# A chip kernel's gathers in two bursts: seven groups, a pause, and then gathers and scatters in turn

## The chip, the cores and the metric

The kernel runs on one core of a Trainium2 chip. The metric is the device time of one execution, in microseconds (us). The engines are PE (matrix products and transposes), ACT, DVE (elementwise work), POOL (here above all the indirect DMAs, each of which POOL issues itself) and SP, whose queue issues the plain DMAs.

## What is computed

`x` has 8192 rows of 256 numbers. The whole is a feed-forward layer with its own attention and a mixture of experts, then a causal self-attention, then the same feed-forward layer again:

```python
x = x + 0.5 * _L0_ffn_ref(_layernorm(x), ...)     # first ffn
x = x + _L0_attn_ref(_layernorm(x), ...)
x = x + 0.5 * _L0_ffn_ref(_layernorm(x), ...)     # second ffn
```

Inside the feed-forward layer, after its attention (`y1`), each row goes to one of 8 experts:

```python
idx = argmax(softmax(y1 @ wg)); loc = position of the row within its expert; keep = loc < cap
h = disp @ w1 + b1;  y = h @ w2 + b2              # per expert, no nonlinearity between
out = where(keep, gate * y[slot], 0)
y2 = layernorm(y1 + out) * ln2_g + ln2_b
```

With nothing nonlinear between `w1` and `w2`, an expert is one 256 x 256 matrix, the product W1W2, and one bias row.

## The kernel before, in words

`ffn` is called twice, with `turn` 0 and 1; the change touches the call with `turn` 0. Each call has three stages.

First `ffn_attention` runs over 16 groups (NG) of 512 rows and stores, for each row, the rows `y1` and `x + ln2_b` side by side in the DRAM scratch `rows`. Then comes the routing: DVE works out each row's slot, and PE turns that into the inverse permutation `inv` (a chain that ends with `s_inv`). In the first call alone, the eight experts' products are formed here too, and go on after the routing is done. Per expert e: PE transposes w1 (`turn_w1`, L1235), ACT copies it out of PSUM (`turned`, L1116), PE multiplies with w2 (`product`, L1246, 32 matmul records), ACT stores the product (`w12_out`, L1121), DVE sums the bias (`bias_product`, L1436 and L1439), PE spreads that sum over the partitions (`bias_sum`, L1277) and DVE adds it (`bias_out`, L1427). `s_w12ps` counts PE's products and `s_acc` DVE's bias sums.

The third stage is the tail, 16 groups of 4 x 128 rows sorted by expert. `gather(n)` issues four indirect DMAs from POOL (L1083) that bring rows of `rows` into `xs[:, n]`; ACT copies them (`place`), PE transposes and multiplies with W1W2 (`products`, L1318), DVE adds and takes the row statistics (`sums`, L1454 to L1473), ACT normalises (L1165), and DVE scales with `ln2_g` and adds (`scale`, L1486 and L1489), which counts up `s_fin`. POOL then scatters the group with four indirect DMAs (L1101) to the place of each row in the output. The stage that follows starts when the last scatter has landed.

The order on each engine is that in which the code is written. On POOL all sixteen gathers stand ahead of all scatters. The buffer `xs` is shared: while the products are formed, the parts 10 and 11 of it hold w1 and the parts 12 to 15 hold w2. Therefore gathers 10 and 11 wait for transposes of w1 (`s_etps`), and gathers 12 to 15 for product and bias sum number n - 7. Each gather from the third on also waits until the one two before it has landed (`got`).

Of the kernel before, what the change touches and what calls it, by code (L numbers as in the profile page):

```python
# [32 lines left out]
NE = 8  # L33
# [898 lines left out]
def ffn(core, name, x, rows, d, w12d, b12d, out, turn, tables):  # L932
# [4 lines left out]
    FB = FF // P  # L937
    CT = TILES // NG * 2
    MINE = (3, 7)
    with Phase(core, name) as ph:  # L940
        logits = ph.sb("logits", [P, TILES, NE])

# [127 lines left out]
        @block.gpsimd  # L1070
        def _(pool):
            nc.gpsimd.iota(ei[:, :], pattern=[[1, NE]], base=0, channel_multiplier=0).then_inc(s_iota, 1)
            nc.gpsimd.iota(ib[:, :], pattern=[[1, P]], base=0, channel_multiplier=0).then_inc(s_ib, 1)
            nc.gpsimd.iota(ni[:, :], pattern=[[1, TILES]], base=0, channel_multiplier=TILES).then_inc(s_ni, 1)
            nc.gpsimd.memset(zero[:, :], 0.0).then_inc(s_zero, 1)
            attend_gpsimd(pool)

            def gather(n):
                if n >= 2:
                    got(pool, n - 2, n % 2)  # L1080
                for t in range(GT):
                    i = n * GT + t
                    pool.indirect_dma_start(xs[:, n, t, :], None, rows,  # L1083
                                            bass.IndirectOffsetOnAxis(ap=inv[:, i:i + 1], axis=0)
                                            ).then_inc(s_got[n % 2], 16)

            for u in range(2):
                stored(pool, u)
            pool.wait_ge(s_inv, 1)
            for n in range(NG):  # L1090
                if turn == 0 and n in (10, 11):
                    pool.wait_ge(s_etps, 4 * (n - 3))
                if turn == 0 and n >= 12:
                    pool.wait_ge(s_w12ps, n - 7)
                    pool.wait_ge(s_acc, n - 7)
                gather(n)
            for n in range(NG):
                pool.wait_ge(s_fin, n + 1)
                for t in range(GT):
                    i = n * GT + t  # L1100
                    pool.indirect_dma_start(out, bass.IndirectOffsetOnAxis(ap=inv[:, i:i + 1], axis=0),  # L1101
                                            xs[:, n, t, 0:C], None).then_inc(s_sent, 16)
            pool.wait_ge(s_sent, sent0 + 16 * TILES)

        @block.scalar
# [1364 lines left out]
```

## Time and profile before

| | us |
|---|---|
| median of 3 runs | 2764.93 |
| lowest and highest | 2763.07 and 2767.3 |
| the profiled execution's own time | 2759.59 |
| its span (first to last instruction) | 2757.9 |
| PE busy in the span | 2334.6 |
| DVE busy | 2151.4 |
| ACT busy | 1657.1 |
| POOL busy | 838.6 |

The first call's routing, products and tail lie between about 488 and 756 us of the span, the second call's tail between 2546 us and the end. A timeline row of the profile gives the start, the length, the engine, the line, the operation and, in brackets, how long the engine was idle before it and what ended that idle time. "issue" there is idle time for which the profile shows nothing that was waited for, and "remote" is a release that it cannot put to an engine of this core.

### The profile page before, as it was taken

The numbers are of one execution on the slowest core, as the hardware profiler recorded it, in microseconds if no ns is written. First come the engines' busy times: TensorE is split into PE (matmuls) and PEld (weight loads), VectorE is DVE, ScalarE is ACT, GpSimd is POOL, SyncE is SP. The second block draws the span as 40 slices with busy tenths as digits, with TensorE's granted clock in tenths as the row PEclk, the third lists the DMA queues.
The fourth block names the chain that finished last, engine by engine and source line by source line (L and its number), as shares of the span: only waits on it lengthen the run. The fifth ranks groups of instructions, "written<-read, shape, count | busy, mean of one in ns | idle before, by whom it ended". The sixth has DMA issues, their size and how long they took to land. (4 is left out here: it accounts for less than half of the span.)

```text
span 2757.9 us, 45893 instructions
## 1 busy us (share of the span) xinstructions
PE 2334.6 (85%) x15352; PEld 1387.7 (50%) x15352; DVE 2151.4 (78%) x5653; ACT 1657.1 (60%) x3995; POOL 838.6 (30%) x853
## 2 busy tenths in 40 slices
PE   5999998877479969999999999999879999994264
PEld 3666665755345524444444444444656666663243
DVE  5888887827778869889889898888458888887077
ACT  3454544416534429999999999999415445452154
POOL 2353433264734430000000000000123343431746
PEclk8999999878889969999999999999989999997677
DMA  4132214283235565445455455452441121211722
GB/s 122 52 97 77 70 47 145 102 271 115 84 126 172 168 126 103 94 102 108 95 106 106 94 105 104 96 107 60 130 153 54 47 69 47 69 47 52 210 73 77
DMA packets 244683, 281.54 MB, mean 102 GB/s; under 512 B 41808, under 2 KB 212880, under 8 KB 243808
## 3 DMA queue, kind: packets, MB, share of 16 engines
q1 hardware_dynamic: 217712, 218.02, 31.1%
q0 software_dynamic: 16384, 50.35, 5.7%
q10 hardware_dynamic: 10352, 10.23, 1.3%
q8 instruction: 123, 2.02, 0.3%
q14 instruction: 112, 0.92, 0.1%
HBM read 190.63 MB, written 94.16 MB: 103 GB/s over the span
## 5 line engine op out<-in xcount | busy, mean ns | idle before, releaser
L2202 DVE CUSTOM_DVE_ANT_0 banks<-banks,attn_bias 128x128 f32<-128x128 f32 (+7 forms) x1024 | 759.7, 778 | 108.1 <-PE banks L1909 82.8
L2115 ACT ACTIVATE attn_probT<-banks 128x512 f32<-128x512 f32 x1152 | 622.5, 621 | 61.2 <-PE banks L1926 50.9
L1909 PE MATMUL banks<-attn_kst,attn_qst 96*128 96x512 bf16 (+3 forms) x1536 | 421.4, 336 | 22.3 <-DMA attn_qst<-qparts 12.3
L1926 PE MATMUL banks<-attn_qst,attn_kst 99*128 99x256 bf16 (+3 forms) x2176 | 410.9, 281 | 15.3 <-ACT attn_probT L2115 7.1
L1948 PE MATMUL banks<-attn_probT,attn_vb 128*32 128x256 f32 (+3 forms) x4352 | 315.6, 400 | 7.9 <-ACT attn_probT L2115 7.3
L1926 PEld LDWEIGHTS banks<-attn_qst,attn_kst 99*128 99x128 bf16 x2176 | 187.3, 97 | 169.3 <-ACT attn_probT L2115 54.9
L2260 POOL CAST attn_lowp<-attn_lowT 128x32 bf16<-128x32 f32 x64 | 13.4, 209 | 850.3 <-DVE attn_lowT L2210 850.3
L410 PE MATMUL banks<-ffn_xT,winT 128*128 128x512 f32 x512 | 250.7, 612 | 6.5 <-ACT ffn_w L610 2.9
L1909 PEld LDWEIGHTS banks<-attn_kst,attn_qst 96*128 96x128 bf16 x1536 | 117.4, 97 | 255.6 <-DVE attn_low L2202 158.1
L2103 ACT COPY banks<-attn_biasT 128x512 f32<-128x512 f32 x384 | 227.8, 628 | 27.9 <-DMA attn_biasT<-neardT 21.2
L870 POOL TENSOR_TENSOR ffn_xs<-ffn_xs,row_ffn_out 128x1024 f32<-128x1024 f32 x32 | 75.4, 2356 | 412.3 <-DVE ffn_xs L752 386.5
L580 ACT ACTIVATE ffn_xs<-banks,ffn_xs 128x128 f32<-128x128 f32 x512 | 182.5, 379 | 12.9 <-DVE ffn_xs L717 11.4
L1948 PEld LDWEIGHTS banks<-attn_probT,attn_vb 128*32 128x32 f32 x4352 | 106.2, 109 | 132.8 <-ACT attn_probT L2115 70.1
L619 ACT COPY ffn_xs<-banks 128x256 f32<-128x256 f32 x128 | 48.2, 377 | 205.3 <-PE banks L459 202.8
L1318 PE MATMUL banks<-ffn_w,ffn_xT 128*128 128x256 f32 x512 | 130.3, 408 | 43.0 <-issue 30.7
L1083 POOL DMA_INDIRECT ffn_xs<-rows,ffn_inv x128 | 122.7, 958 | 141.5 <-DVE ffn_inv L1423 90.5
L610 ACT ACTIVATE ffn_w<-banks,ffn_qk_b 64x512 f32<-64x512 f32 x128 | 87.3, 682 | 125.7 <-PE banks L410 124.9
L717 DVE TENSOR_REDUCE ffn_xs<-banks 128x4 f32<-128x512 f32 x128 | 88.4, 691 | 86.8 <-PE banks L439 86.5
L2202 DVE DVE_READ_ACCUMULATOR2_ANT attn_low<- 128x1 f32 x1024 | 143.8, 140 | 0.1
L725 DVE TENSOR_SCALAR ffn_xs<-ffn_xs 128x128 f32<-128x128 f32 x512 | 138.4, 332 | 4.5
L439 PE MATMUL banks<-ffn_w,ffn_xs 128*128 128x256 f32 x512 | 141.1, 400 | 0.8 <-DVE ffn_xs L739 0.8
L410 PEld LDWEIGHTS banks<-ffn_xT,winT 128*128 128x128 f32 x512 | 90.3, 192 | 93.3 <-issue 73.8
(254 smaller groups left out, 4507.9 us busy)
## 6 DMA issues: line engine op xcount, KB each, us to landing
rows<-ffn_xs SPq DMA_DIRECT2D x64, 512.0 KB, 3.1
attn_qst<-qparts SPq DMA_DIRECT2D x384, 64.0 KB, 2.8
attn_kst<-kparts SPq DMA_DIRECT2D x186, 128.0 KB, 5.0
ffn_xs<-in_L_ffn_w_dram SPq DMA_DIRECT2D x16, 1024.0 KB
attn_biasT<-neardT SPq DMA_DIRECT2D x128, 128.0 KB, 5.0
attn_bias<-neard SPq DMA_DIRECT2D x128, 128.0 KB, 2.2
qparts<-qkv_part SPq DMA_DIRECT2D x32, 384.0 KB, 2.8
kparts<-qkv_part SPq DMA_DIRECT2D x32, 384.0 KB, 2.8
```

What stands on the lines that cost most here:

```text
L410: mm = nc.tensor.matmul(bank[QK], core.winT[:, k, j * P:(j + 1) * P], xT[:, u, k, :], start=(k == 0), stop=(k == KB - 1))
L439: mm = nc.tensor.matmul(bank[SC[t % 2]][:, 2 * j * P:(2 * j + 2) * P].rearrange("p (h c) -> p h c", h=2), qT[:, u, j, t * P:(t + 1) * P], ...
L580: ins = nc.scalar.activation(prob[:, t % 2, h, :], bank[SC[t % 2]][:, h * P:(h + 1) * P], ACT.Exp, bias=negm[:, t % 2, h:h + 1], scale=1.0 ...
L725: ins = nc.vector.tensor_scalar(prob[:, t % 2, h, :], prob[:, t % 2, h, :], rinv[:, t % 2, h:h + 1], None, ALU.mult)
L1083: pool.indirect_dma_start(xs[:, n, t, :], None, rows, bass.IndirectOffsetOnAxis(ap=inv[:, i:i + 1], axis=0)).then_inc(s_got[n % 2], 16)
L1318: mm = nc.tensor.matmul(part, xT[:, u, k, t * P:(t + 1) * P], w12[:, k, expert(n, u)], start=False, stop=(k == KB - 1), skip_group_check=True)
L1909: mm = nc.tensor.matmul(score[k % 2][:, a:e], qst[0:K6, u, half, hh, ii * P:(ii + 1) * P], kst[0:K6, u, hh, a:e], start=True, stop=True)
L1926: mm = nc.tensor.matmul(tbank[t % 3][:, at:at + nb * P], kst[:, u, hh, j * P:(j + 1) * P], qst[:, u, half, hh, x:x + nb * P], start=(k == ...
L1948: mm = nc.tensor.matmul(obank[32 * hh:32 * hh + 32, x:x + nb * P], vb[:, u, j, hh, :], probT[:, g % 2, i, at:at + nb * P], start=hh not in ...
L2103: nc.scalar.copy(tbank[t % 3].rearrange("p (a c) -> p a c", a=2), over(near[:, 0:2 * P], 2, 1)).then_inc(s_seed, 1)
L2115: nc.scalar.activation(probT[:, g % 2, i, 0:w], tbank[t % 3][:, 0:w], ACT.Exp, scale=-1.0).then_inc(s_exp, 1)
L2202: nc.vector.tensor_tensor_reduce(out=part, in0=part, in1=bias[:, hh, T - w:T], scale=1.0, scalar=BIG, op0=ALU.add, op1=ALU.min, accum_out= ...
```

## The change

In the first call the gathers of groups 0 to 6 are issued as before. Then POOL waits for the eighth product and the eighth bias sum. After that it issues the gathers of groups 7 to 12, scatter 0, gather 13, scatter 1, gather 14, scatter 2, gather 15, scatter 3, and then scatters 4 to 15. The waits of gathers 10 to 15 on single transposes and products go away, since the one wait covers them. In the second call `AHEAD` is 16, and its order is as before.

```diff
     CT = TILES // NG * 2
     MINE = (3, 7)
+    AHEAD = (12, NG)[turn]
...
-            for u in range(2):
-                stored(pool, u)
-            pool.wait_ge(s_inv, 1)
-            for n in range(NG):
-                if turn == 0 and n in (10, 11):
-                    pool.wait_ge(s_etps, 4 * (n - 3))
-                if turn == 0 and n >= 12:
-                    pool.wait_ge(s_w12ps, n - 7)
-                    pool.wait_ge(s_acc, n - 7)
-                gather(n)
-            for n in range(NG):
+            def scatter(n):
                 pool.wait_ge(s_fin, n + 1)
                 for t in range(GT):
                     i = n * GT + t
                     pool.indirect_dma_start(out, bass.IndirectOffsetOnAxis(ap=inv[:, i:i + 1], axis=0),
                                             xs[:, n, t, 0:C], None).then_inc(s_sent, 16)
+
+            for u in range(2):
+                stored(pool, u)
+            pool.wait_ge(s_inv, 1)
+            for n in range(NG):
+                if turn == 0 and n == 7:
+                    pool.wait_ge(s_w12ps, NE)
+                    pool.wait_ge(s_acc, NE)
+                gather(n)
+                if n >= AHEAD:
+                    scatter(n - AHEAD)
+            for n in range(NG - AHEAD, NG):
+                scatter(n)
             pool.wait_ge(s_sent, sent0 + 16 * TILES)
```

On POOL, before the change, these rows are gathers 9 to 12 of the first call; each group is one row with its waits (`indirect0` and `indirect1` are the landings of earlier gathers) and one row for its other three DMAs.

```order
L1083 DMA ffn_xs<-rows,ffn_inv 128x512 [waits indirect1]
L1083 DMA ffn_xs<-rows,ffn_inv 128x512 x3
L1083 DMA ffn_xs<-rows,ffn_inv 128x512 [waits indirect0,ffn1_etps]
L1083 DMA ffn_xs<-rows,ffn_inv 128x512 x3
L1083 DMA ffn_xs<-rows,ffn_inv 128x512 [waits indirect1,ffn1_etps]
L1083 DMA ffn_xs<-rows,ffn_inv 128x512 x3
L1083 DMA ffn_xs<-rows,ffn_inv 128x512 [waits indirect0,ffn1_acc,ffn1_w12ps]
L1083 DMA ffn_xs<-rows,ffn_inv 128x512 x3
```

On POOL after the change, gathers 6 to 8 of the first call:

```order
L1084 DMA ffn_xs<-rows,ffn_inv 128x512 [waits indirect0]
L1084 DMA ffn_xs<-rows,ffn_inv 128x512 x3
L1084 DMA ffn_xs<-rows,ffn_inv 128x512 [waits indirect1,ffn1_acc,ffn1_w12ps]
L1084 DMA ffn_xs<-rows,ffn_inv 128x512 x3
L1084 DMA ffn_xs<-rows,ffn_inv 128x512 [waits indirect0]
L1084 DMA ffn_xs<-rows,ffn_inv 128x512 x3
```

The wait on the product and the bias sum has moved from gather 12 to gather 7, and it is now for number 8, where gather 12 waited for number 5; no gather behind it has such a wait.

The second place is the end of the gathers on POOL. Before, it is gather 15 and then scatters 0 and 1:

```order
L1083 DMA ffn_xs<-rows,ffn_inv 128x512 [waits indirect1,ffn1_acc,ffn1_w12ps]
L1083 DMA ffn_xs<-rows,ffn_inv 128x512 x3
L1101 DMA x<-ffn_xs,ffn_inv 8192x256 [waits ffn1_fin]
L1101 DMA x<-ffn_xs,ffn_inv 8192x256 x3
L1101 DMA x<-ffn_xs,ffn_inv 8192x256 [waits ffn1_fin]
L1101 DMA x<-ffn_xs,ffn_inv 8192x256 x3
```

After the change, on POOL, it is gather 12, scatter 0, gather 13, scatter 1 and gather 14:

```order
L1084 DMA ffn_xs<-rows,ffn_inv 128x512 [waits indirect0]
L1084 DMA ffn_xs<-rows,ffn_inv 128x512 x3
L1092 DMA x<-ffn_xs,ffn_inv 8192x256 [waits ffn1_fin]
L1092 DMA x<-ffn_xs,ffn_inv 8192x256 x3
L1084 DMA ffn_xs<-rows,ffn_inv 128x512 [waits indirect1]
L1084 DMA ffn_xs<-rows,ffn_inv 128x512 x3
L1092 DMA x<-ffn_xs,ffn_inv 8192x256 [waits ffn1_fin]
L1092 DMA x<-ffn_xs,ffn_inv 8192x256 x3
L1084 DMA ffn_xs<-rows,ffn_inv 128x512 [waits indirect0]
L1084 DMA ffn_xs<-rows,ffn_inv 128x512 x3
```

Scatter 0 has moved ahead of gathers 13 to 15, which thereby stand behind its wait on `s_fin`. The rows of the other engines stand in the same order before and after.

## Rows read from the trace of the kernel before

**Rows 1.** Busy time by stretch: engines, granted PE clock, DMA share, GB/s.

```profile
core 0: us, PE busy (x) PEld busy (x) DVE busy (x) ACT busy (x) POOL busy (x), PEclk, DMA share, GB/s
580.00:590.00 10.00, 6.20 (x13) 3.10 (x13) 0.00 (x0) 0.00 (x0) 7.56 (x9) 0.50 0.76 242
590.00:600.00 10.00, 3.99 (x7) 2.06 (x7) 0.00 (x0) 0.58 (x1) 7.01 (x8) 0.50 0.72 210
```

**Rows 2.** Timeline of PE during the products of the first call.

```profile
546.96 7.07 PE L1246 MATMUL banks<-ffn_xs,ffn_xT 128*128 128x256 f32 x32
...
584.77 1.98 PE L1246 MATMUL banks<-ffn_xs,ffn_y 128*128 128x256 f32 x3
...
601.59 6.74 PE L1246 MATMUL banks<-ffn_xs,ffn_y 128*128 128x256 f32 x18 [0.81 <-issue]
...
608.60 7.07 PE L1246 MATMUL banks<-ffn_xs,ffn_xT 128*128 128x256 f32 x32
```

**Rows 3.** Timeline of POOL: gathers of the first call.

```profile
539.34 1.44 POOL L1083 DMA_INDIRECT ffn_xs<-rows,ffn_inv  x1 [46.62 <-DVE ffn_inv L1423]
...
578.20 0.95 POOL L1083 DMA_INDIRECT ffn_xs<-rows,ffn_inv  x1 [0.30 <-issue]
...
598.19 0.94 POOL L1083 DMA_INDIRECT ffn_xs<-rows,ffn_inv  x1 [0.30 <-issue]
603.42 0.94 POOL L1083 DMA_INDIRECT ffn_xs<-rows,ffn_inv  x1 [4.29 <-remote]
...
622.68 0.95 POOL L1083 DMA_INDIRECT ffn_xs<-rows,ffn_inv  x1 [0.30 <-issue]
628.45 0.94 POOL L1083 DMA_INDIRECT ffn_xs<-rows,ffn_inv  x1 [4.82 <-issue]
```

**Rows 4.** Timeline of ACT: copies of products out of PSUM.

```profile
598.10 0.58 ACT L1121 COPY ffn_w<-banks 128x512 f32<-128x512 f32 x1 [23.41 <-remote]
...
620.56 0.59 ACT L1121 COPY ffn_w<-banks 128x512 f32<-128x512 f32 x1 [9.72 <-remote]
```

**Rows 5.** Timeline of DVE: bias sums of the products.

```profile
603.23 0.43 DVE L1427 TENSOR_TENSOR ffn_b<-banks,ffn_b 128x256 f32<-128x256 f32 x1 [24.06 <-remote]
...
623.38 0.42 DVE L1427 TENSOR_TENSOR ffn_b<-banks,ffn_b 128x256 f32<-128x256 f32 x1 [10.24 <-remote]
...
624.10 3.61 DVE L1439 SCALAR_TENSOR_TENSOR ffn_acc<-ffn_xs,b1T,ffn_acc 128x256 f32<-128x256 f32 x7
```

**Rows 6.** Timeline of DVE in the first tail.

```profile
653.81 1.23 DVE L1489 TENSOR_TENSOR ffn_xs<-ffn_xs 128x1024 f32<-128x1024 f32 x1
...
659.07 1.22 DVE L1486 TENSOR_TENSOR ffn_xs<-ffn_xs,row_ln_g 128x1024 f32<-128x1024 f32 x1
660.32 1.22 DVE L1489 TENSOR_TENSOR ffn_xs<-ffn_xs 128x1024 f32<-128x1024 f32 x1
...
743.78 1.24 DVE L1489 TENSOR_TENSOR ffn_xs<-ffn_xs 128x1024 f32<-128x1024 f32 x1
```

**Rows 7.** Timeline of POOL: scatters of the first tail.

```profile
655.32 1.01 POOL L1101 DMA_INDIRECT x<-ffn_xs,ffn_inv  x1 [22.17 <-DVE ffn_xs L1489]
...
659.19 1.94 POOL L1101 DMA_INDIRECT x<-ffn_xs,ffn_inv  x1 [0.30 <-issue]
...
742.49 0.97 POOL L1101 DMA_INDIRECT x<-ffn_xs,ffn_inv  x1 [0.30 <-issue]
...
755.23 0.97 POOL L1101 DMA_INDIRECT x<-ffn_xs,ffn_inv  x1 [0.30 <-issue]
```

**Rows 8.** Timeline of POOL, second tail: first and last of 64 gathers.

```profile
2547.20 1.09 POOL L1083 DMA_INDIRECT ffn_xs<-rows,ffn_inv  x1 [43.92 <-DVE ffn_inv L1423]
...
2626.12 0.94 POOL L1083 DMA_INDIRECT ffn_xs<-rows,ffn_inv  x1 [0.30 <-issue]
```

**Rows 9.** Timeline of DVE in the second tail.

```profile
2571.35 0.87 DVE L1460 SCALAR_TENSOR_TENSOR ffn_xs<-banks,ffn_gnow,ffn_xs 128x256 f32<-128x256 f32 x2
2592.01 0.88 DVE L1460 SCALAR_TENSOR_TENSOR ffn_xs<-banks,ffn_gnow,ffn_xs 128x256 f32<-128x256 f32 x2 [19.79 <-remote]
...
2634.77 0.17 DVE L1454 COPY ffn_gnow<-ffn_gates 128x4 f32<-128x4 f32 x1 [39.83 <-remote]
```

## The prediction, made before the changed kernel had run

> **What bounds the kernel now.** I read the shares by stretch first, because the change touches one engine's order in one stage, and what matters is what each engine does between the end of the routing (538 us) and the end of the first tail (756 us). From 580 to 600 us [rows 1] POOL issues gathers at full pace, while DVE has no instruction and ACT one. PE runs 20 matmuls in these 20 us, at the 1.2 GHz level of its clock (0.50), and the DMA engines are not full (0.72 to 0.76). So neither a busy engine nor bandwidth holds these 20 us.
>
> The timelines of the engines say what it is. A product of 32 matmuls takes 7.07 us at 547 and at 608 us; the one begun at 584.77 ends only at 608 us [rows 2], over 23 us. ACT's store of a product comes at 598.10 after 23.41 us idle [rows 4]; DVE's next bias add comes at 603.23 after 24.06 us idle [rows 5]. "Issue" and "remote" mean that no engine's work was late. What does fit is the gather stream: POOL issues the 44 gathers of groups 0 to 10 from 539.34 and ends the last at 599.13, waits 4.29 us itself, and goes on at 603.42 [rows 3]. DVE and PE are back to full pace within the same four microseconds. It recurs: the 16 gathers of groups 11 to 14 run from 603.42 to 623.63, ACT's last store waits from the product's end (608.60 + 7.07 = 615.67) to 620.56, and DVE's bias add until 623.38 [rows 2 to 5]. The second tail shows it at its largest: 64 gathers in a row from 2547.20 to 2627.06 [rows 8], and DVE stands 19.79 and 39.83 us in them, until 2634.77 [rows 9]. I read this as: a long unbroken stream of gathers stops the other engines' instructions after a while, and they come back about 4 us (7.7 after the long stream) after it ends.
>
> The tail itself is bound by DVE: group 0 is finished at 655.04, group 1 at 661.54, so 6.5 us a group, and group 15 at 745.02 [rows 6]. POOL's last scatter ends at 756.20 [rows 7], and the next stage waits for it.
>
> **The change, step by step** (in the profiled execution's own time).
>
> *The pause.* Gather 27, the last of group 6, ends at 578.20 + 0.95 = 579.15 [rows 3]. Ending there takes 16 gathers out of the stream, 1.25 us apart (578.20 to 598.19 is 16 of them). If the engines recover 4 us later, as at 603, they are back at 583.2. The bounds are 579 (at once) and 586.9 (7.7 us). From there PE does the end of the bias sum (0.7), the product (7.07), a bias sum (0.4), the last product (7.07) and a bias sum (0.6): 599.0. DVE follows with one bias add (0.4) and the last bias product, which before began 0.34 us after 623.38 and ended at 624.10 + 3.61 = 627.71 [rows 5], 4.33 us in all: 603.3. So the eighth bias sum moves from 627.7 to 603.3, 24.4 us earlier (20.7 to 28.5). ACT's copies (0.6 each) and SP's two stores of the products to DRAM lie beside this; the stores then flow while POOL is silent or in its first gathers.
>
> *What is behind the new wait.* Gathers 7 to 15 and with them every scatter. POOL starts 0.74 us after the bias sum, as it did at 628.45: 604.0. Six groups are 24 gathers x 1.25 = 30 us, to 634.0. Before, only gather 15 was still to be issued at this point. This is the price of the pause: 32 more gathers, 40 us of POOL's time, lie behind that point.
>
> *The tail's start.* DVE finished group 0 at 655.04, 27.3 us after the last bias sum; unhindered that is 630.6. Scatter 0 could then go at 634. But from 604 to 634 POOL streams gathers without a break. In the second tail, which also began after a rest, DVE stopped at 2572.2, 25 us after the first gather [rows 8, 9]. The same here is 629, just short of group 0's end. POOL then stands at scatter 0's wait from 634 on, the stream is broken, 4 us later (638) the engines are back, and group 0's last steps take 2 to 3 us. I take scatter 0 at 641; the ends are 635 (no stop, and DVE in POOL's way once) and 655 (rival C).
>
> *From scatter 0 to the end.* POOL now has 16 scatter groups and 3 gather groups, one after another: 16 x 5.10 (the ten steps from 742.49 to 755.23 are 1.274 each [rows 7], so 5.10 a group) + 3 x 5.0 = 96.6 us. The scatter at 659.19, which started 0.12 us into DVE's two-input multiply, took 1.94 us instead of 0.97; that at 742.49, started just before one, took 0.97 [rows 6, 7]. So each of some 14 groups that DVE still finishes may cost POOL nothing to 1.0 us; I take 12 us in all, with 0 and 14 as the ends. That is 108.6 us from scatter 0 to the last scatter's end, where before it was 756.20 - 655.32 = 100.9. DVE, at 6.5 us a group, needs only 90 us from group 0 to group 15, so POOL is the bound, and a stop of DVE by up to 15 us in the middle would be hidden.
>
> The Trainium skill, page "SBUF — State Buffer", section "Who interferes with whom", says that a DVE instruction with two SBUF inputs contends only with a GpSimd instruction that reads SBUF, and supposes that writing descriptors needs the other interface. By that the twelve microseconds would be 0 and the end that much earlier. The scatter at 659.19 doubled, and our gathers and scatters read their indices from SBUF, so the trace decides for the cost.
>
> *Sum.* 641 + 108.6 = 749.6 against 756.2: 6.6 us less. The stages behind only move. From the profiled execution's 2759.6 this gives 2753.0; the median of the runs is 2764.9, 5.3 above it, and I carry the difference over: **2758.3 us**.
>
> **The rivals.**
>
> *A, no second stop.* Scatter 0 goes at 635, and the end is 635 + 108.6 = 743.6, 12.6 us less: 2752.3. For it: group 0 needs only until 630.6, and DVE in the second tail still worked 25 us after the first gather. Against it: that same 25 us.
>
> *C, the second burst stops the tail for long.* In the first call the second stream made ACT late after 12.3 us (603.42 to 615.67), though after a rest of only 4 us. If DVE stops 12.3 us into the new burst, at 616.3, then 14.3 us of work remain before group 0 is done (630.6); the engines return at 638 to 641.7, so scatter 0 goes at 652.3 to 656: the end is 761 to 765, that is 5 to 8 us slower, around 2771.5. A further stop under the alternating stream, beyond the 15 us of cover, would come on top. It decides from the point where scatter 0 comes later than 756.2 - 108.6 = 647.6; the burst itself is over at 634.
>
> *D, the gathers are not what stops the engines.* Then the last bias sum stays at 627.7, gather 7 starts at 628.4, scatter 0 at 628.4 + 30 + 1 = 659.5, and the end is 768, 12 us slower: 2776.8. For it: at 547 a product takes its 7.07 us beside gathers. Against it: three stops, each ending within 8 us of a stream's end. The Trainium skill, page "SBUF — State Buffer", section "SBUF: two separate sides", says that a DMA cannot be slowed by a compute instruction nor the reverse; by that rule this rival would hold and its 12 us with it. The trace disagrees as far as a product of 23 us beside gathers, against 7.07, can show it.
>
> *E, gain and price cancel for another reason*, such as scatters that land late: 2764.9.
>
> **How the numbers follow.** A change of 0.2% is 5.5 us, about what a measurement of this kernel can tell from none. The forecast (a short second stop, 1 to 10 us gained) has 0.42, its own range 2755 to 2764; 0.25 of it is faster and 0.17 the same. A has 0.21, faster. C has 0.23: 0.07 the same, 0.16 slower. D has 0.12, slower, and E 0.02. Together 0.46 faster, 0.26 the same, 0.28 slower. Leaving out D with the far end of C (0.14) and A's far end, where the recovery is instant and DVE costs POOL nothing (0.05), the range is 2749 to 2773.
>
> **What would show it.** Right: PE runs both last products at 7.07 us from about 583; the eighth bias sum ends near 603; POOL idles about 24 us after gather 6 and is then never idle over 2 us from scatter 0 on; DVE's group 15 is done some 20 us before POOL's last scatter. The second stop shows as "remote" on DVE or ACT between 622 and 640 and as POOL's wait ahead of scatter 0. Wrong if PE still has its gaps from 583 to 601 with POOL silent (D), if DVE stands over 12 us in the burst (C), or if scatter 0 goes at 635 (A). Most exposed is the length of the second stop: each microsecond of it beyond 634 is one of the sum.

## The result, and the profile after

| us | before | changed |
|---|---|---|
| median of 6 runs each, on one chip | 2766.11 | 2773.59 |
| lowest and highest | 2758.11 and 2768.0 | 2772.57 and 2778.2 |
| the profiled execution's own time | 2759.59 | 2773.26 |
| its span | 2757.9 | 2771.5 |
| PE / DVE / ACT / POOL busy | 2334.6 / 2151.4 / 1657.1 / 838.6 | 2338.3 / 2153.6 / 1657.3 / 836.2 |
| last scatter of the first tail ends | 756.20 | 767.92 |

The changed kernel is slower: the ratio is 1.0032, with the 95% interval 1.0022 to 1.0041. The busy times are the same within 4 us, so no work was added. Of the 13.6 us by which the span is longer, 11.7 are there when the first tail ends. The second call's code is unchanged, and its tail is nearly so: 202.6 us for 203.2, with stops of DVE of 19.66 and 36.82 us for 19.79 and 39.83 [rows 9].

These are rows of POOL's timeline in the changed kernel: the gathers (L1084) and scatters (L1092) of the first call at which something begins or ends.

```profile
577.58 0.94 POOL L1084 DMA_INDIRECT ffn_xs<-rows,ffn_inv  x1 [0.30 <-issue]
601.53 0.95 POOL L1084 DMA_INDIRECT ffn_xs<-rows,ffn_inv  x1 [23.01 <-DVE ffn_acc L1443]
...
630.26 0.95 POOL L1084 DMA_INDIRECT ffn_xs<-rows,ffn_inv  x1 [0.30 <-issue]
645.91 1.01 POOL L1092 DMA_INDIRECT x<-ffn_xs,ffn_inv  x1 [14.71 <-DVE ffn_xs L1493]
...
652.36 1.88 POOL L1084 DMA_INDIRECT ffn_xs<-rows,ffn_inv  x1 [0.30 <-issue]
...
681.86 0.97 POOL L1092 DMA_INDIRECT x<-ffn_xs,ffn_inv  x1 [0.31 <-issue]
692.87 0.97 POOL L1092 DMA_INDIRECT x<-ffn_xs,ffn_inv  x1 [10.04 <-DVE ffn_xs L1493]
...
766.95 0.97 POOL L1092 DMA_INDIRECT x<-ffn_xs,ffn_inv  x1 [0.30 <-issue]
```

They answer to [rows 3] and [rows 7]. POOL is silent for 23.01 us, as the new wait asks, issues the 24 gathers of groups 7 to 12 from 601.53 to 631.21, and then waits 14.71 us for DVE's group 0. From 645.91 to 682.83 it issues 28 DMAs of both kinds without a gap. Then it waits once more, 10.04 us, for DVE's group 4.

This is PE's timeline during the pause (L1250 is the product, L1281 the bias sum), and one row of the second burst and three from the end of the mixed stream of gathers and scatters.

```profile
581.58 7.07 PE L1250 MATMUL banks<-ffn_xs,ffn_y 128*128 128x256 f32 x32
...
588.92 7.07 PE L1250 MATMUL banks<-ffn_xs,ffn_xT 128*128 128x256 f32 x32
...
625.57 4.18 PE L1322 MATMUL banks<-ffn_w,ffn_xT 128*128 128x256 f32 x9 [6.52 <-issue]
...
681.69 0.38 PE L1322 MATMUL banks<-ffn_w,ffn_xT 128*128 128x256 f32 x1 [0.88 <-issue]
683.09 0.38 PE L1322 MATMUL banks<-ffn_w,ffn_xT 128*128 128x256 f32 x1 [1.03 <-issue]
684.49 0.59 PE L1322 MATMUL banks<-ffn_w,ffn_xT 128*128 128x256 f32 x1 [1.02 <-issue]
```

With POOL silent both last products take 7.07 us each, where one begun at 584.77 took over 23 us before [rows 2]. In the burst PE stands again for 6.52 us and gets through 9 matmuls in 4.18 us. The last three rows show that a "stop" is not always a standstill: PE runs single matmuls, 1.40 us apart, though nothing that the profile shows holds it.

DVE's timeline shows the rest: the last bias product, the row behind which the second stop begins, that stop's end, the last operation of group 0, and the same pair for a third stop with the end of group 4 behind it.

```profile
597.18 3.61 DVE L1443 SCALAR_TENSOR_TENSOR ffn_acc<-ffn_xs,b1T,ffn_acc 128x256 f32<-128x256 f32 x7
...
616.51 0.22 DVE L1477 TENSOR_SCALAR ffn_ve<-ffn_mv 128x4 f32<-128x4 f32 x1
634.93 0.17 DVE L1458 COPY ffn_gnow<-ffn_gates 128x4 f32<-128x4 f32 x1 [18.20 <-remote]
...
644.41 1.22 DVE L1493 TENSOR_TENSOR ffn_xs<-ffn_xs 128x1024 f32<-128x1024 f32 x1
...
652.18 1.22 DVE L1490 TENSOR_TENSOR ffn_xs<-ffn_xs,row_ln_g 128x1024 f32<-128x1024 f32 x1
...
670.54 1.23 DVE L1493 TENSOR_TENSOR ffn_xs<-ffn_xs 128x1024 f32<-128x1024 f32 x1
685.99 0.17 DVE L1458 COPY ffn_gnow<-ffn_gates 128x4 f32<-128x4 f32 x1 [14.22 <-remote]
...
691.37 1.23 DVE L1493 TENSOR_TENSOR ffn_xs<-ffn_xs 128x1024 f32<-128x1024 f32 x1
```

The eighth bias product ends at 600.79 (627.71 before). From 616.73 DVE stands 18.20 us, until 3.7 us after the burst's last gather has ended, and group 0 is done at 645.63. It stands again 14.22 us, until 3.2 us after the mixed stream's last DMA has ended at 682.83, so that group 4 is done at 692.60, 20.8 us after group 3. Not all of this is DVE's own: by the program the row at L1458 waits for PE's products of the next group, and in the third stop PE took from 676.63 to 687.76 for 16 matmuls that took 3.69 us at 663.46. Before the change DVE did stand by itself: PE's bias sum was done at 584.65, and the add that waited for it came at 603.23 [rows 5].

The busy time by stretch in the changed kernel (columns as in [rows 1]) puts the pause beside the two later stops.

```profile
580.00:601.00 21.00, 17.72 (x90) 15.47 (x90) 12.57 (x29) 6.68 (x11) 0.00 (x0) 1.00 0.23 94
616.00:635.00 19.00, 7.94 (x26) 5.10 (x25) 0.73 (x7) 3.22 (x6) 11.56 (x13) 0.77 0.66 191
662.00:683.00 21.00, 11.37 (x44) 8.71 (x43) 5.67 (x16) 7.12 (x14) 15.96 (x17) 0.76 0.49 151
```

In the pause PE runs 90 matmuls with its clock granted at the 2.4 GHz level (1.00), in place of the 20 at 0.50 before. In the second stretch the pattern of [rows 1] is back: POOL busy, all the others mostly standing. In the third it is weaker: PE is still busy 11.37 of the 21 us, DVE 5.67. The DMA engines are at 0.66 and 0.49 of their time, further from full than before. What the pause took out of the middle of the routing came back twice in the tail.

### The profile page after: what moved, and what is told of

The parts are those of the page before. It is cut to its first block and busy times, and to the rows that moved or that the text cites. A ratio compares the mean times of both kernels' runs of the same rounds, so it can differ in the third digit from the quotient of the medians.

```text
span 2771.5 us, 45886 instructions
## 1 busy us (share of the span) xinstructions
PE 2338.3 (84%) x15350; PEld 1392.6 (50%) x15352; DVE 2153.6 (78%) x5653; ACT 1657.3 (60%) x3995; POOL 836.2 (30%) x853
## 5 line engine op out<-in xcount | busy, mean ns | idle before, releaser
L2264 POOL CAST attn_lowp<-attn_lowT 128x32 bf16<-128x32 f32 x64 | 13.4, 209 | 851.0 <-DVE attn_lowT L2214 851.0
L1322 PE MATMUL banks<-ffn_w,ffn_xT 128*128 128x256 f32 x512 | 141.0, 429 | 57.4 <-issue 47.0
L1084 POOL DMA_INDIRECT ffn_xs<-rows,ffn_inv x128 | 123.2, 963 | 155.8 <-DVE ffn_inv L1427 90.7
L1322 PEld LDWEIGHTS banks<-ffn_w,ffn_xT 128*128 128x128 f32 x512 | 108.1, 217 | 82.6 <-issue 53.4
```

The lines of the kernel that those rows point to most:

```text
L1084: pool.indirect_dma_start(xs[:, n, t, :], None, rows, bass.IndirectOffsetOnAxis(ap=inv[:, i:i + 1], axis=0)).then_inc(s_got[n % 2], 16)
L1322: mm = nc.tensor.matmul(part, xT[:, u, k, t * P:(t + 1) * P], w12[:, k, expert(n, u)], start=False, stop=(k == KB - 1), skip_group_check=True)
```

## The experiments

Two theories stood first. **S**: an unbroken stream of POOL's indirect DMAs stops PE, ACT and DVE after some time, wherever in the program it runs, and they return when it ends. **P**: the stops belong to places of the program and have a length of their own. Later **W** was added: the pause is POOL time thrown away, which costs even where nothing is stopped. "Order" is the sequence of gathers and scatters on POOL. Each ratio is to the kernel before on the same chip, and where one edit is given as "the change's lines", the diff of the change stands there unaltered but for what is shown. A trace is of one execution, and executions of one kernel differ: those of e1 by 11.5 us. The traced executions of e1, e2 and e4 are slow ones (2773.15, 2777.96 and 2777.22 us, 4 to 6 above the medians), so their places in a trace are compared with the changed kernel's (2773.26) only roughly. From the first gather to the end of the last scatter the first tail takes 216.9 us before, 229.2 with the change, 230.5 in e1, 233.6 in e2, 232.8 in e3, 234.4 in e4 and 215.6 in e8.

**e1: the pause alone.** The waits of the change, and all gathers ahead of all scatters.

```diff
+    AHEAD = NG
```

> The pause alone: the wait ahead of gather 7 stays, all sixteen gathers stand ahead of the scatters again. Theory S (an unbroken gather stream stops the other engines until about 4 us after it ends): the second stream is now 36 gathers, 601.5 to 646.5 us; DVE stands from about 617 to 650, group 0 is done near 661, the tail is bound by DVE behind that, and the last scatter ends near 762 (767.9 in the changed kernel, 756.2 before): a time of about 2772. Theory P (the engines run out of instructions at fixed places of the program and the length of the stop is that of a fetch, whatever POOL does): DVE stands 18 us at the same instruction as in the changed kernel, group 0 is done near 646, last scatter near 747: a time of about 2757.

Measured: 2767.56, ratio 1.0023 [1.0011, 1.0035]. The last 36 gathers run from 602.10 to 646.9, and the last scatter ends at 767.5. These rows of e1's DVE timeline are its stops in them. (An idle time of 12.03 us that ended at 615.52 is mostly the ordinary wait for group 0's products; it is 8.51 us in e9, where nothing stops.)

```profile
625.28 0.88 DVE L1464 SCALAR_TENSOR_TENSOR ffn_xs<-banks,ffn_gnow,ffn_xs 128x256 f32<-128x256 f32 x2 [8.68 <-issue]
...
652.70 0.17 DVE L1458 COPY ffn_gnow<-ffn_gates 128x4 f32<-128x4 f32 x1 [24.49 <-remote]
```

The same work on DVE, the row at L1458, is let go at 634.93 with 24 gathers and at 652.70 with 36: the end of the stop moves with the end of the stream (+3.7 and +5.8 us). That speaks against P. The end, expected 6 us before the changed kernel's, came as late as that in this trace (767.5 and 767.9): scatter 0 goes only at 663.69, where 645.91 is the changed kernel's, and from it to the end it is 103.8 us, near the 100.9 of before. The trace is the slowest of e1's ten executions; by the medians the pause alone costs 6 us.

**e2: the turns alone.** `AHEAD` and `scatter` of the change, but the old waits of gathers 10 to 15.

```diff
             for n in range(NG):
                 if turn == 0 and n in (10, 11):
                     pool.wait_ge(s_etps, 4 * (n - 3))
...
                 gather(n)
+                if n >= AHEAD:
+                    scatter(n - AHEAD)
```

> The alternation alone: gathers 7 to 15 have their old waits, and scatters 0 to 3 stand between gathers 12 to 15. Theory S: the stop from 580 to 603 us comes back, but the stream behind 603 is only 8 gathers long, so the one of 616 to 623 falls away; the eighth bias sum comes near 620, group 0 near 648, and then the mixed stream of 16 scatters and 12 gathers stops the engines once more for about 13 us: last scatter near 769, a time of about 2779. Rival (the mixed stream stops them only because the burst came just before): no stop there, last scatter near 757, a time of about 2767.

Measured: 2774.02, ratio 1.0041 [1.0026, 1.0055], the last scatter ends at 774.4. Rows of e2's DVE and then POOL timelines:

```profile
699.23 0.17 DVE L1460 COPY ffn_gnow<-ffn_gates 128x4 f32<-128x4 f32 x1 [10.01 <-remote]
...
706.10 0.97 POOL L1092 DMA_INDIRECT x<-ffn_xs,ffn_inv  x1 [9.65 <-DVE ffn_xs L1495]
```

Without any pause, and with scatter 0 at 653.46, near the 655.32 of before, gathers and scatters in turn (653.5 to 696.5) stop DVE, and POOL then waits 9.65 us for it. This is the changed kernel's third stop without the burst ahead of it, so the rival falls, and it is the step that the prediction had taken as harmless. The turns alone cost about 11 us (0.0041 of 2762), the pause alone 6 and both together 9. The stop is not all of the 11: from scatter 0 to the end e2 takes 121.0 us for 100.9, and the twelve gathers that now stand behind scatter 0 are 15 of POOL's time by themselves.

**e3: half the bytes.** The change's lines, and the gathers of groups 7 to 15 fetch rows of 1 KB, half their size. It leaves out the second half of those rows (ln2's shift and the residual); the computation behind goes on with zeros or old numbers there.

```diff
+                half = turn == 0 and n >= 7
...
-                    pool.indirect_dma_start(xs[:, n, t, :], None, rows,
+                    pool.indirect_dma_start(xs[:, n, t, 0:C] if half else xs[:, n, t, :], None, x if half else rows,
```

> The changed kernel, with gathers 7 to 15 of the first call fetching 1 KB a row (from x) in place of 2 KB (from rows), so that the second half of those groups is not loaded; the number of DMAs, of rows and of descriptors is the same. If bytes moved make the stop, none or a much shorter one comes in the second burst (24 gathers) and in the mixed stream: scatter 0 near 632, last scatter near 741, a time of about 2746. If the number of gathers or rows makes it, DVE stands about 18 and 14 us as in the changed kernel and the time stays near 2773.

Measured (one run): 2777.69, the last scatter ends at 773.0. Rows of e3's DVE timeline:

```profile
626.38 0.88 DVE L1469 SCALAR_TENSOR_TENSOR ffn_xs<-banks,ffn_gnow,ffn_xs 128x256 f32<-128x256 f32 x2 [7.97 <-remote]
...
639.16 0.17 DVE L1463 COPY ffn_gnow<-ffn_gates 128x4 f32<-128x4 f32 x1 [9.85 <-remote]
...
697.57 0.17 DVE L1463 COPY ffn_gnow<-ffn_gates 128x4 f32<-128x4 f32 x1 [11.37 <-remote]
```

The busy time of a stretch of e3's burst, and of one of e7, where the gathers are spaced and nothing stops (columns as in [rows 1]):

```profile
618.00:632.00 14.00, 4.48 (x22) 3.77 (x21) 3.24 (x13) 1.14 (x2) 10.65 (x12) 0.71 0.37 104
...
600.00:620.00 20.00, 18.98 (x79) 13.44 (x79) 8.53 (x31) 8.85 (x16) 15.04 (x27) 0.87 0.85 292
```

The stops sum to 17.8 us in the burst, as long as the changed kernel's 18.20, at 104 GB/s and a DMA share of 0.37; in e7 PE is busy 18.98 of 20 us beside 292 GB/s and a share of 0.85. So it is not the bytes and not how full the DMA engines are. What is left is the number of DMAs, or of the rows in them, which e3 leaves as it was: these two were not told apart. Scatters, which carry 1 KB a row too, fit that.

**e4: the last three gather groups spread out.** The waits of the change, and gathers 13, 14 and 15 behind scatters 3, 6 and 9.

```diff
+                for n in range(NG):
+                    scatter(n)
+                    if n in (3, 6, 9):
+                        gather(12 + n // 3)
```

> The changed kernel with gathers 13, 14 and 15 moved behind scatters 3, 6 and 9 in place of 0, 1 and 2. POOL has the same work from scatter 0 on, but one gather group for three or four scatter groups. Theory S with a share (scatters count little): the burst's stop stays (scatter 0 near 646), the second stop goes, POOL works through in 108.6 us, last scatter near 754.5: a time of about 2760. Rival (any unbroken work of POOL stops the engines, scatters as much as gathers): a stop of some 14 us stays, somewhere in 662 to 700, last scatter at 760 to 768, a time of 2766 to 2773.

Measured: 2772.7, ratio 1.0032 [1.0018, 1.0046], the last scatter ends at 774.7. A miss: I had expected it to be as fast as before, and the rival came true. A row of e4's DVE timeline, and two of its POOL timeline:

```profile
709.90 0.17 DVE L1464 COPY ffn_gnow<-ffn_gates 128x4 f32<-128x4 f32 x1 [8.57 <-remote]
...
716.77 0.97 POOL L1092 DMA_INDIRECT x<-ffn_xs,ffn_inv  x1 [9.49 <-DVE ffn_xs L1499]
...
752.17 0.96 POOL L1092 DMA_INDIRECT x<-ffn_xs,ffn_inv  x1 [7.55 <-DVE ffn_xs L1499]
```

The stops came later and in smaller pieces, and POOL waited 9.49 and 7.55 us all the same. Scatters without a gap count as well; which of the two kinds is issued makes no difference that these runs show.

**e5, e6: two rests behind each gather DMA.** The order of before; behind each indirect DMA of a gather, POOL writes two tiles of 128 x 128 and waits for each, so that the DMAs are mostly 1.70 us apart in place of 1.25 (1.84 and 1.86 on average, since DVE and landings hold some up): in the first call (e5), in both (e6).

```diff
+            def rest(times):
+                for _ in range(times):
+                    nc.gpsimd.memset(filler[:, :], 0.0).then_inc(s_filled, 1)
+                    filled[0] += 1
+                    pool.wait_ge(s_filled, filled[0])
...
+                    if turn == 0:
+                        rest(2)
```

> The kernel before with its old order, and after each gather DMA of the first call two small POOL memsets with a wait on each, so that the gathers come some 1.7 us apart in place of 1.25. Theory B (the engines stop when POOL's DMAs have run at full pace for some 15 to 25 us; a rest of 4 to 8 us, or a share of POOL's issuing under about three quarters, keeps them free): no stop of over 5 us between 560 and 650; the eighth bias sum at about 600, gathers until about 650, scatters until about 742, a time 14 us below before. Rival N (the stops follow the number of gathers issued, not their pace): the stops stay, the gathers end 25 to 30 us later, and the time is 15 to 25 us above before.

> The same pace in both calls. Theory B: in the second tail, too, DVE no longer stands 20 and 40 us; it works at 6.5 us a group behind gathers that end about 112 us after their start (2659 on the old scale), the scatters end near 2750 in place of 2758: a time about 7 us below that of the first call's pace alone, and 20 below before. Rival N: the second tail grows by the 30 us of added POOL time.

Measured: e5 2762.97, ratio 0.9984 [0.9975, 0.9994]; e6 2763.21, ratio 0.9986 [0.9976, 0.9995]. The gather stops went as expected, the times did not: 4 us below before in both, for 14 and 20. In e5 DVE has no idle time over 6 us that ends in "remote" or "issue" while gathers are issued (539 to 656), and group 0 is done at 622.8, where it was 655.04. Only POOL is late now: the gathers end at 656, and the scatters follow without a gap. Rows of e5's DVE and then POOL timelines:

```profile
714.39 0.17 DVE L1465 COPY ffn_gnow<-ffn_gates 128x4 f32<-128x4 f32 x1 [16.95 <-remote]
...
721.45 0.97 POOL L1112 DMA_INDIRECT x<-ffn_xs,ffn_inv  x1 [11.67 <-DVE ffn_xs L1500]
```

The scatters from 657.5 to 709.8 stop DVE for 16.95 us: scatters alone do it. The stops are cured in the gathers at a price of at least 0.45 us for each of 64 DMAs, 29 us, which eats most of the gain.

**e7: one rest behind each gather DMA, both calls.** As e6 with `rest(1)`, mostly a DMA every 1.45 us (1.54 and 1.56 on average).

> Both calls, with one memset after each gather DMA: some 1.5 us apart, a share of about 0.83. Theory B: stops come later and are shorter than before but not gone; a time between before and the slower pace, 5 to 15 us below before. Rival N: 10 to 15 us above before in each call.

Measured: 2739.47, ratio 0.9893 [0.9875, 0.9911]. The first tail's gathers begin at 542.04, and the last scatter ends at 744.1: 202.1 us, where before it is 216.9 [rows 3, 7]. The second goes from 2535.7 to 2731.0, 195.3 us for 203.2. The time is 28 us below before, more than the 5 to 15 expected, and apart from the ordinary wait for group 0 DVE has no idle time of over 6.1 us left under the gathers; the stops that are left, up to 16.78 us, fall under the scatters, which have no rests. That a slower POOL makes the kernel 1% faster is the strongest sign for S.

**e8: a shorter pause.** The change's order; gather 7 waits for the seventh product only, and 12 to 15 have their old waits.

```diff
+                if turn == 0 and n == 7:
+                    pool.wait_ge(s_w12ps, NE - 1)
```

> The changed kernel, with gather 7 waiting for the seventh product (about 589) in place of the eighth and its bias sum (601), and the old waits back on gathers 12 to 15: a rest of 11 us in place of 23. Theory B (rest beyond some 8 us buys nothing): the eighth bias sum stays near 601, the second stream runs from 589 to 619 and stops DVE until about 623, group 0 is done near 641 in place of 645.6, the last scatter near 763 in place of 767.9: a time about 5 us below the changed kernel. Rival (the whole rest is needed, and each microsecond less costs one more of stop): the bias sum comes late by 5 to 10 us and the time is that of the changed kernel or above.

Measured: 2763.75, ratio 0.9991 [0.9982, 1.0001]. POOL's timeline in e8, gather 7, scatter 0, scatter 4 and the last scatter:

```profile
592.17 0.94 POOL L1084 DMA_INDIRECT ffn_xs<-rows,ffn_inv  x1 [10.60 <-PE banks L1252]
...
635.15 1.01 POOL L1092 DMA_INDIRECT x<-ffn_xs,ffn_inv  x1 [9.56 <-DVE ffn_xs L1495]
...
682.14 0.97 POOL L1092 DMA_INDIRECT x<-ffn_xs,ffn_inv  x1 [9.72 <-DVE ffn_xs L1495]
...
756.34 0.97 POOL L1092 DMA_INDIRECT x<-ffn_xs,ffn_inv  x1 [0.30 <-issue]
```

With 10.60 us of pause and a second gap ahead of 609.81, scatter 0 goes at 635.15 and the end is at 757.31, 10.6 us before the changed kernel's. The eighth bias product ended at 604.05, for 600.79 with the whole pause, and no stop of over 5 us fell into the burst behind it; two breaks in that burst, where POOL waited 2.44 and 1.35 us for landings, may have helped, which is not shown. The wait for group 4 behind the mixed stream (9.72) is still there. So this order with a short pause is as fast as the order of before, within the interval, and no faster.

**e9: one rest behind each scatter DMA as well.** As e7, both calls.

```diff
+                    rest(1)
```

> The kernel before with one memset rest after each gather and after each scatter, in both calls. Theory B (POOL's scatters stop the engines as its gathers do): the stop of DVE of 8.9 us that the run with rests after the gathers alone had under its run of scatters (660 to 680) goes; DVE then sets the pace at 6.5 us a group behind 4 scatters in 5.9 us, and the time is equal to that run's or up to 5 us below. Rival (scatters are harmless, POOL is simply busy): each tail grows by most of 64 x 0.2 us, and the time is 12 to 25 us above that run.

Measured: 2746.12, ratio 0.9938 [0.9922, 0.9955], 12 us above e7 by the ratios: the stops went as theory B has it, the time is the rival's. Three rows of POOL's timeline in e9 in the first tail:

```profile
700.34 0.98 POOL L1111 DMA_INDIRECT x<-ffn_xs,ffn_inv  x1 [0.28 <-POOL ffn_filler L1083]
...
701.82 0.98 POOL L1111 DMA_INDIRECT x<-ffn_xs,ffn_inv  x1 [0.28 <-POOL ffn_filler L1083]
...
703.29 1.68 POOL L1111 DMA_INDIRECT x<-ffn_xs,ffn_inv  x1 [0.28 <-issue]
```

DVE now has no stop in either tail from group 0 on, and POOL is never idle for long: its scatters, 1.48 us apart and more where DVE blocks one, set the end: the two tails take 203.8 and 199.7 us (541.69 to 745.45, 2539.57 to 2739.25), where e7's take 202.1 and 195.3. The stop is cured, and the time is lost to the cure.

**e10: the change's order with one rest behind each gather DMA, both calls.** The change's lines and e7's rests.

> The changed kernel with one memset rest after each gather, in both calls; it stands against the kernel before with the same rests. If the pause of 23 us is wasted issuing time once the stream no longer stops anyone, scatter 0 goes near 636, POOL has 3 gather groups and 16 scatter groups behind it, and the first tail ends 5 to 12 us after that of the run with the old order: a time 5 to 12 us above it, still some 15 us below before. If the change's order is of use on its own, the time is equal to that run's or below.

Measured: 2733.87, ratio 0.9896 [0.9877, 0.9915]. The first tail takes 538.25 to 751.20, 213.0 us, against e7's 202.1 for the old order. The ratio is e7's all the same, where 5 to 12 us more was expected, because the second tail, whose code is the same in both, takes 183.1 in e10 and 195.3 in e7. So tails with the same code differ by as much as 12 us from one kernel to another, and comparing single calls needed the runs below.

**e11: four rests behind each group, both calls.** The order of before; the rests of e7 stand together, behind the group's fourth DMA.

```diff
                                             ).then_inc(s_got[n % 2], 16)
+                rest(GT)
```

> The kernel before with the same number of rests, but four behind the fourth gather DMA of a group, in place of one behind each DMA: the same share of POOL's issuing over a group. If the share counts over many DMAs, the time is within 4 us of the run with one rest each. If it is the spacing of one DMA to the next that keeps the engines free, the stops come back and the time is near that of before.

Measured: 2729.69, ratio 0.9886 [0.9869, 0.9902], the lowest of all, though its interval overlaps those of e7 and e10. POOL's timeline in e11, one group of gathers and the last scatter of the first tail:

```profile
591.64 0.95 POOL L1092 DMA_INDIRECT ffn_xs<-rows,ffn_inv  x1 [0.50 <-POOL ffn_filler L1083]
...
594.15 1.19 POOL L1092 DMA_INDIRECT ffn_xs<-rows,ffn_inv  x1 [0.30 <-issue]
595.64 0.95 POOL L1092 DMA_INDIRECT ffn_xs<-rows,ffn_inv  x1 [0.30 <-issue]
596.59 1.00 POOL L1083 MEMSET ffn_filler<- 128x128 f32 x4
598.09 0.95 POOL L1092 DMA_INDIRECT ffn_xs<-rows,ffn_inv  x1 [0.50 <-POOL ffn_filler L1083]
...
741.39 0.97 POOL L1111 DMA_INDIRECT x<-ffn_xs,ffn_inv  x1 [0.30 <-issue]
```

Four DMAs and their rests take 6.45 us in this piece (591.64 to 598.09), 0.24 of it because DVE holds one up, so some 1.55 each. How the rest is dealt out, by DMA or by group, makes no difference beyond the intervals (0.9893 and 0.9886, in two calls), even at a step of 1.25 us within a group; what counts is how many DMAs there are over a longer stretch.

**e12: the smallest rest.** As e7, but the tile written is one element wide, a DMA mostly every 1.33 us (1.45 and 1.38 on average).

```diff
+        filler, s_filled = tile("filler", 1), ph.sem("filled")
```

> The kernel before with a rest after each gather DMA whose memset is one element wide (0.1 us): a step of about 1.33 us in place of 1.45 and 1.25. Theory B: a stop that builds up more slowly than before and is not gone; the time lies between before and the run at 1.45, 10 to 20 us below before. If a threshold at some spacing decides, the time is that of the run at 1.45, or that of before.

Measured: 2747.31, ratio 0.9955 [0.9932, 0.9978]. Two rows of e12's DVE timeline:

```profile
604.52 0.42 DVE L1437 TENSOR_TENSOR ffn_b<-banks,ffn_b 128x256 f32<-128x256 f32 x1 [12.76 <-remote]
...
634.33 0.17 DVE L1464 COPY ffn_gnow<-ffn_gates 128x4 f32<-128x4 f32 x1 [14.88 <-remote]
```

It lies between: the stops of 24.06 us and more are shorter but there. But the median hides two outcomes: six of e12's ten executions took 2739.5 to 2750.5 us, 13 to 24 below the median of before (2763.1), and four took 2759.4 to 2762.3, hardly less than before. The trace is of one of the six. Under gathers a step of 1.25 us stops the engines, 1.33 less or not always, 1.45 and 1.70 no longer, beyond idle times of 6.1 us and the ordinary wait for group 0.

What was still open then: does the change lose even where the gather stream stops nothing (W), and is it its pause or its turns? Three kernels have e11's rests in the first call alone and so the second call of before.

```diff
+                if turn == 0:
+                    rest(GT)
```

**e13** has the order of before, **e14** that of the change, **e15** the pause of the change with all gathers first (`AHEAD = NG`).

> The kernel before with four memset rests behind each gather group, in the first call alone; the second call is as before. From the run with these rests in both calls (its first tail took 202 us from the first gather to the last scatter, 217 before): 15 us below before, a ratio near 0.9946.

> The same rests in the first call alone, with the changed kernel's order. Theory W (the pause takes POOL's time, and POOL's DMA issuing bounds the tail from the last bias sum on, stops or not): the eighth bias sum near 597, 24 gathers at 1.56 us to 636, then 16 scatter and 3 gather groups: last scatter 8 to 12 us after that of the old order with rests, so 3 to 7 us below before, a ratio of 0.998. Rival M (only the stops made the change slow): the same time as the old order with rests, a ratio near 0.9946.

> The same, with the pause and all sixteen gathers ahead of the scatters. Theory W: POOL has the same work behind the pause, so within 4 us of the changed order with rests. If the turns of gathers and scatters are what costs there, this run is as fast as the old order with rests.

| | median | ratio | first gather to end of last scatter |
|---|---|---|---|
| e13, old order | 2748.84 | 0.9951 [0.9935, 0.9968] | 539.80 to 745.11: 205.3 |
| e14, changed order | 2754.3 | 0.9973 [0.9964, 0.9983] | 541.59 to 753.73: 212.1 |
| e15, pause, gathers first | 2758.0 | 0.9983 [0.9974, 0.9993] | 539.21 to 754.26: 215.1 |

A row of e14's POOL timeline, the end of the pause, one of its DVE timeline, and two of POOL's again, its wait for DVE and its last scatter:

```profile
598.75 0.95 POOL L1093 DMA_INDIRECT ffn_xs<-rows,ffn_inv  x1 [13.04 <-DVE ffn_acc L1454]
...
717.16 0.17 DVE L1469 COPY ffn_gnow<-ffn_gates 128x4 f32<-128x4 f32 x1 [20.41 <-remote]
...
724.03 0.96 POOL L1103 DMA_INDIRECT x<-ffn_xs,ffn_inv  x1 [9.86 <-DVE ffn_xs L1504]
...
752.76 0.97 POOL L1103 DMA_INDIRECT x<-ffn_xs,ffn_inv  x1 [0.30 <-issue]
```

The same wait of POOL in e13:

```profile
689.79 0.97 POOL L1112 DMA_INDIRECT x<-ffn_xs,ffn_inv  x1 [10.19 <-DVE ffn_xs L1500]
```

The rests make the first tail of the changed order 17.0 us shorter (212.1 for 229.2) and that of the old order 11.6 (205.3 for 216.9), so a part of what the change lost went with the gather stops. The old order is still 5.5 us ahead of the change's and 9.2 ahead of the pause's by the medians, 6.8 and 9.7 by the tails. The intervals of e13 and e15 lie apart, so W holds for the pause; those of e13 and e14 overlap at their ends (0.9968 and 0.9964), so for the change it holds with less certainty: about 6 of its 9 us remain. The stop under the scatters does not make the difference, since POOL waits as long for DVE in e13 (10.19) as in e14 (9.86). The lost POOL time does: in e15 the last gather begins 11.3 us later than in e13, and POOL idled 13.27 us in the pause. Whether the turns give back anything (e14 against e15) the overlapping intervals leave open.

## Why the prediction went wrong, point by point

**Right.** *The pause* ended the stop at once: PE was back by 580 us (583.2 forecast), ran both products at 7.07, and the eighth bias product ended at 600.79 (603.3). POOL idled 23.0 us (24). The 24 gathers took 29.7 us (30). Rival D, that gathers are not the cause, fell with this, and the rule by which it would hold, from the Trainium skill, page "SBUF — State Buffer", section "SBUF: two separate sides" (a DMA does not slow a compute instruction), does not fit as a forecast: e7 and e11 change nothing but how densely POOL issues, and gain 1.1%. No run shows that the SBUF's ports, of which the section speaks, are the place.

*POOL's own price* of the tail was right too. From scatter 0 to the end, 96.6 us of issuing were forecast, and 12 for DMAs that DVE holds up; the second measured 8.2 from scatter 4 on (the excess of the DMAs over 0.97 us each), and some 1.5 before it, within its bounds of 0 and 14. The gather at 652.36 that took 1.88 us began 0.18 us into DVE's multiply at 652.18, as the scatter of [rows 7] did. The Trainium skill, page "SBUF — State Buffer", section "Who interferes with whom", supposes that writing descriptors is not held up by such a multiply. The trace disagrees for these DMAs; they also read their indices from SBUF, and no run tells whether it is that reading or the writing that waits.

**Mis-sized: the second stop.** The prediction let DVE stop 25 us into the burst, "just short of group 0's end", and resume at 638. It stopped at 616.73, 15 us in, and resumed at 634.93. That lies between the forecast and rival C (12.3 us). By the prediction's own sign, DVE standing over 12 us in the burst, it is rival C; by the other, scatter 0 later than 647.6, it just is not: 645.91 for 641, which is 4.9 us. The 25 us came from the second tail, which follows a long silence of POOL; here 23 us of silence gave 15. The prediction also took the first stream of 44 gathers as unbroken, and it is not: POOL waits 2.20, 1.49 and 1.33 us for landings in it (ahead of 551.98, 563.28 and 574.31).

**The step that failed** is "a stop of DVE by up to 15 us in the middle would be hidden", and with it the picture of the mixed stream as a break. DVE stopped at 671.77 for 14.22 us, below 15, and was not hidden, because the cover had not yet been built up: at that point POOL was to be done with scatter 3 at 682.83, and DVE's group 4 would have been done 6.5 us after group 3, at 678.3. The cover was 4.5 us, so POOL waited 9.7 of the 14.2. Group 3 was late by some 4 us already, with DVE waiting 3.93 us for PE ahead of 666.15. Later waits at DVE's pace, the largest of 1.97 us, add 6.0. Two of the prediction's signs of being right failed here: POOL was to be never idle over 2 us from scatter 0 on, and idled 10.04; DVE's group 15 was to be done some 20 us before the last scatter, and was done 11 us before it. From scatter 0 to the end 96.6 + 9.7 + 8.2 + 1.5 + 6.0 = 122.0 us were measured for 108.6 forecast, 13.4 more. Beneath the cover lies a second error: where POOL is the bound, its stream is unbroken, and an unbroken stream is what stops DVE (scatters alone do in e5, spaced ones do not in e9). Before the change DVE set the pace, four scatters in 6.5 us or 1.63 us each, and it had no stop over 5 us in that stretch.

**The sum** was 749.6 for the last scatter, and is 767.9: 4.9 + 13.4 = 18.3. Against the 756.20 of before, it is 11.7 us slower. Rival C had named what came, "a further stop under the alternating stream ... would come on top", but without a number and without a chance of its own. The median, 2773.59, lies 0.6 above the range.

**Why the old order loses less than it seems.** In the old order the same stops fall into the routing, and at the end of it POOL has only one group of gathers left. While DVE catches up, 22.17 us [rows 7], POOL is silent, at a place where only scatters are left to be issued. The change puts 23.01 us of rest ahead, where they hold up 36 gathers, and still has 14.71 ahead of scatter 0. That this is why the old order loses less is a reading of the two traces; e13 and e15 bear it out for the pause. Short breaks behind every group of gathers (e11) cost 0.3 us a DMA (1.55 for 1.25) and make the kernel some 32 us shorter over both calls.

**Open.** What in the chip stops the engines is not settled. It is not the bytes (e3), not the DMA engines being full (a share of 0.37 in e3's stop, 0.85 without a stop in e7), not a place in the program (e1). The number of DMAs, or of their rows, in a stretch fits all runs; at which point of their way they hold up the other engines was not tried. The traces cannot tell POOL's issuing from the moving of the rows: the last packets of the changed kernel's burst end near 633.4, between POOL's last issue (631.21) and DVE's return (634.93), and those of the mixed stream near 683.8 (682.83 and 685.99). How long a stream may run before the stop begins was 12 to 26 us in these traces, and 33 us in the changed kernel's first stream with its short waits (PE has gaps from 571.9 on, the first gather is at 538.77). It depends on what went before; I have no rule that gives it. And the 12 us by which the second tail varies with the same code (e7, e10) is unexplained.

## What to carry to other kernels

Where several engines idle at once with no releaser that fits, look for the one that does not, and test it by slowing it down: a rest of 0.2 us after each of POOL's gathers, some 16% of its pace, made this kernel 1.1% faster. A long pause does not do the same, since the saving ends with the pause, while everything queued behind it is late. And a margin at the end of a pipeline is no margin in its middle: count it at the place where the stop will fall, and count with the stream in it: where the issuing engine is the bound, its stream has no breaks left.

## What the runs showed that was not expected

- Scatters stop the other engines as gathers do: 16.95 us for DVE under scatters alone (e5), 20.41 us in e14, where the last gathers, with rests, stand among the scatters.
- The engines come back 3 to 6 us after POOL's last DMA of the stream has ended (3.2, 3.7, 5.8 us; 7.7 after the 64 gathers of the second tail).
- The pace decides within narrow limits, in the commonest step between gather DMAs: 1.25 us gives ratio 1, 1.33 gives 0.9955 (two outcomes, see e12), 1.45 gives 0.9893, and 1.70 gives 0.9986, since then POOL itself is late.
- A DMA from POOL that begins within 0.4 us of the start of a DVE multiply with two inputs of 128x1024 ends about 2.06 us after that start, 0.84 us after the multiply's end: 0.06 us in, it takes 2.00 us (696.69 in the changed kernel), 0.18 in 1.88, 0.39 in 1.68 (703.29 in e9), in place of 0.95 to 0.97.
